# A two-stage graph network on one core: each graph layer sums its messages over the edge counts before the weight product, and the product out2 @ Wu is made of high and low parts

## What is computed

```python
# first stage
out1 = gat_conv(layer_norm(x), ..., W1, ...)          # 4 heads of 192
out2 = gat_conv(out1, ..., W2, ...)                   # 2 heads of 96
l0   = concatenate([x, out2], -1) @ Wu + bu
x1   = _layernorm(x + l0)
# second stage: gcn_conv twice
def gcn_conv(x, W, b):
    h = x @ W
    norm = dinv[src] * dinv[dst]                      # dinv = 1/sqrt(degree)
    return segment_sum(h[src] * norm[:, None], dst) + b
h   = relu(gcn_conv(x1, gW1, gb1))
out = _layernorm(x1 + gcn_conv(h, gW2, gb2))
```

## Time and profile before

| | |
|---|---|
| median of 3 runs | 818.07 us (817.19 to 819.74) |
| span of the profiled execution | 818.5 us |
| PE busy | 781.8 us, 96% |
| weight loads busy | 656.0 us, 80% |
| VectorE busy | 583.6 us, 71% |
| ScalarE busy | 301.9 us, 37% |
| GpSimd busy | 19.9 us, 2% |
| mean granted TensorE clock | 0.988 |

### The profile page before, as it was taken

One profiled execution on the slowest core, in us unless ns is written; L12 is line 12 of the kernel. 1 busy time (PEld: TensorE's weight loads), 2 busy tenths in 40 slices (PEclk: granted clock), 3 DMA queues, 4 the chain that ended last, 5 costly groups with the idle time before them and its releaser, 6 DMA issues. The chain is left out here.

```text
span 818.5 us, 11911 instructions
## 1 busy us (share of the span) xinstructions
PE 781.8 (96%) x4286; PEld 656.0 (80%) x4286; DVE 583.6 (71%) x1145; ACT 301.9 (37%) x622; POOL 19.9 (2%) x36
## 2 busy tenths in 40 slices
PE   5999999998999999999998999899999999999997
PEld 4966666665666989999766887788898889999997
DVE  2599997885999999999689998966616432113444
ACT  4546576654534334444154454222212311110000
POOL 6100000000000020000000000000000000000000
PEclk9999999999899999999999999999999999999999
DMA  9400000000000131010000500000021000000111
GB/s 310 155 2 1 1 2 1 1 2 1 1 1 0 66 131 65 1 65 1 1 0 22 188 1 2 1 1 1 1 99 38 1 1 1 1 1 20 59 58 54
DMA packets 10541, 27.78 MB, mean 34 GB/s; under 512 B 665, under 2 KB 4075, under 8 KB 9968
## 3 DMA queue, kind: packets, MB, share of 16 engines
q1 hardware_dynamic: 10480, 26.97, 9.4%
HBM read 23.09 MB, written 3.88 MB: 33 GB/s over the span
## 5 line engine op out<-in xcount | busy, mean ns | idle before, releaser
L1190 PE MATMUL ps<-g,att 128*128 128x193 f32 x800 | 133.5, 328 | 3.2 <-DVE att L662 1.8
L1190 PEld LDWEIGHTS ps<-g,att 128*128 128x128 f32 x800 | 130.4, 190 | 6.0 <-DVE att L662 3.3
L1025 ACT ACTIVATE att<-att,ssrc 128x1250 f32<-128x1250 f32 x60 | 80.2, 1338 | 97.8 <-DVE att L701 97.5
L701 DVE SCALAR_TENSOR_TENSOR att<-uB,s 128x1250 f32<-128x1250 f32 x60 | 90.4, 1511 | 0.0
L1190 PE MATMUL ps<-wp,xT 128*128 128x388 f32 x240 | 87.5, 502 | 0.8 <-ACT xT L908 0.8
L662 DVE SCALAR_TENSOR_TENSOR att<-att,ct 128x1250 f32<-128x1250 f32 x60 | 87.2, 1455 | 0.7 <-ACT att L1025 0.5
L1190 PE MATMUL ps<-yhi,ctr 128*128 128x384 f32 x200 | 67.7, 338 | 0.0
L1190 PEld LDWEIGHTS ps<-wp,xT 128*128 128x128 f32 x240 | 42.6, 190 | 24.8 <-issue 1.0
L765 DVE SCALAR_TENSOR_TENSOR ylo_a<-ps,dinv,yhi 128x384 fp32r<-128x384 f32 x32 | 18.9, 615 | 57.5 <-ACT yhi L883 57.4
L883 ACT ACTIVATE yhi<-ps,dinv 128x384 fp32r<-128x384 f32 x40 | 22.1, 580 | 86.8 <-PE ps L1190 86.8
L1190 PE MATMUL ps<-ylo_a,ctr 128*128 128x384 f32 x160 | 54.1, 338 | 0.0
(11 more groups left out here) (259 smaller groups left out, 1445.4 us busy)
## 6 DMA issues: line engine op xcount, KB each, us to landing
uB<-u_dram SPq DMA_DIRECT2D x4, 1280.0 KB, 6.0
wux<-in_L_gnn_Wu SPq DMA_DIRECT2D x2, 2304.0 KB, 15.7
gw<-in_L_gnn_W SPq DMA_DIRECT2D x2, 2304.0 KB, 10.9
xs<-in_x SPq DMA_DIRECT2D x1, 3456.0 KB
out<-ybuf SPq DMA_DIRECT2D x9, 384.0 KB, 2.3
w<-in_L_gnn_W SPq DMA_DIRECT2D x2, 1152.0 KB, 6.9
w2x<-in_L_gnn_W SPq DMA_DIRECT2D x1, 576.0 KB, 7.7
wuo<-in_L_gnn_Wu SPq DMA_DIRECT2D x1, 576.0 KB
```

Source lines behind the costliest of these rows:

```text
L701: v.scalar_tensor_tensor(att[:, att_place(n), 0:N], uB[:, hp % 2, 1, 0:N], s08[:, h, q:q + 1], uB[:, hp % 2, 0, 0:N], ALU.add, ALU.max).th ...
L1025: a.activation(at_, at_, ACT.Exp, bias=ssrc[:, h, q:q + 1]).then_inc(att_exp, 1)
L1190: return t.matmul(o, lhsT, rhs, start=start, stop=stop, **kw)
```

## The change

**Order of the layers.** Each layer sums its messages first and multiplies by the weights afterwards. The message of a tile is the normalised tile times dinv (`message_high` on ScalarE, `message_low` on VectorE); it has nodes on partitions already, so x1 is not transposed any more. The sums come out transposed and are split at once (`sums_high`, `sums_low`). The product with gW1 then has nodes on partitions, so the bias is a row that is broadcast (`gb1b`), and `degree_rows`, `sqB` and `dinv2` are not used. The last product before the epilogue is now h-sums @ gW2, 18 products for each half instead of 20.

**Order on PE at the start.** Per tile: `o_half`, the transposes of the next tile, `o_half`, then `pair` of the tile two before (LAG = 2), which sums slices 0 and 1 of the features. Slice 2 is summed for tiles 0 to 7 after that, then tiles 8 and 9 for slices 0 to 2, then slices 3 to 5. The wide branch is taken ahead of all this.

**out2 @ Wu.** Six fp32r products for each half of a tile in place of two plain fp32 ones. ScalarE makes the high parts of the weights in the last attention head, GpSimd the low parts; VectorE makes `o2Tlo`.

**Engines.** Widening the counts moves from VectorE to ScalarE. The low part of gW1 moves behind slice 2 of the sums. The ranges of windows are held as 16-bit integers.

```diff
+LAG = 2
+A_BANKS = [(2, 3, 4), (6, 7, 4), (0, 1, 5), (2, 3, 4), (6, 7, 0), (1, 5, 2)]
@@ sync
-            sp.wait_ge(y_ps, 2 * T)
+            sp.dma_start(gb1b[:, :], t_in["L1_gnn_b1"]...to_broadcast([P, D])).then_inc(gcn_in, 16)
+            sp.dma_start(gb2b[:, :], t_in["L1_gnn_b2"]...to_broadcast([P, D])).then_inc(gcn_in, 16)
+            sp.wait_ge(h_ps, 2 * T)
             sp.dma_start(gw2[:, :, :], ...)
@@ gpsimd
+            pool.wait_ge(wuo_hi, 2)
+            pool.tensor_tensor(wuolo[0:HC, 0, :], wuo[0:HC, 0, :], wuohi[0:HC, 0, :], ALU.subtract)
+            pool.tensor_tensor(wuolo[0:HC + 1, 1, :], wuo[0:HC + 1, 1, :], wuohi[0:HC + 1, 1, :], ALU.subtract)
@@ vector
+                o2t_low(0)
                 for q in range(T):
+                    residual(q)                 # two adds, o2t_low(q + 1) between them
+                    if q > 0:
+                        normalised(q - 1)
+                    variance(q)
+                    if q > 0:
+                        message_low(q - 1)
+                normalised(T - 1)
+                message_low(T - 1)
                 for f in range(KD):
+                    sums_low(f, a_place, ahi_out, alo_out)
+                    if f == 2:
+                        first_weight_low(0, KD)
@@ scalar
+                    if hp == H1 + 1 and q < 2:
+                        if q == 0:
+                            a.wait_ge(wuo_in, 32)
+                        copy(wuohi[0:HC + q, q, :], wuo[0:HC + q, q, :], wuo_hi)
+                o2_transposes(0)
+                o2_transposes(1)
+                count_tile(0)
+                count_tile(1)
+                deviation(0)
+                o2_transposes(2)
                 for q in range(T):
+                    message_high(q)
                     if q + 1 < T:
+                        deviation(q + 1)
                     if q + 3 < T:
                         o2_transposes(q + 3)
+                    count_tile(...)
+                def sums_high(f, place, sums_ps, done, last):
+                    a.wait_ge(sums_ps, last)    # last = max(3 * f + 3, 6) in the first layer
+                    for k, (c0, c1) in enumerate(PIECES):
+                        copy(yhi[...], place(f, k), done)
@@ tensor
-                mm(ps[:, k, 0:HALF], o2T[0:HC, ...], wuo[0:HC, 0, ...], True, False)
-                mm(ps[:, k, 0:HALF], o2T[0:HC + 1, ...], wuo[0:HC + 1, 1, ...], False, True)
+                for o in range(H2):
+                    mm(ps[:, k, 0:HALF], o2Thi[0:rows, q % 2, o, :], wuohi[0:rows, o, cols], o == 0, False)
+                    mm(ps[:, k, 0:HALF], o2Thi[0:rows, q % 2, o, :], wuolo[0:rows, o, cols], False, False)
+                    last = mm(ps[:, k, 0:HALF], o2Tlo[0:HC, q % 2, o, :], wuohi[0:HC, o, cols], False, o == 1)
+                for q in range(1, T):
+                    o_half(q, 0)
+                    if q + 1 < T:
+                        o2_transposes(q + 1)
+                    o_half(q, 1)
+                    if q >= LAG:
+                        pair(q - LAG)
+                for q in range(T - LAG):
+                    sums(2, q)
+                for q in range(T - LAG, T):
+                    pair(q)
+                    sums(2, q)
+                for f in range(3, KD):
+                    for q in range(T):
+                        sums(f, q)
```

More of the change, by code:

```diff
@@ L760, in _, with messages, o2t_low, residual @@
             v.wait_ge(att_used, (H1 + H2) * T)
[L762 to L768, removed]
-                steps = n_own[0]
[L771 to L775, removed]
+            def messages(y):
+                steps = n_own[0]
+                def o2t_low(q):
+                    v.wait_ge(o2t_out, q + 1)
+                    v.tensor_tensor(o2Tlo[0:HC, q % 2, :, :], ps[0:HC, 5, 0:2 * P].rearrange("p (o n) -> p o n", o=2),
+                                    o2Thi[0:HC, q % 2, :, :].bitcast(F32), ALU.subtract).then_inc(o2tlo_out, 1)
+                def residual(q):
                     for k in range(2):
+                        if k == 1 and q + 1 < T:
+                            o2t_low(q + 1)
                         v.wait_ge(o_ps, 2 * q + k + 1)
@@ L852, in first_end @@
+                hidden_low(2 * T - 1)
+                for f in range(KD):
+                    sums_low(f, b_place, bhi_out, blo_out)
+                    if f == 1:
                         for c in range(KD):
@@ new lines, in messages @@
+                for n in range(2 * T):
+                    q, k = n // 2, n % 2
+                    a.wait_ge(h_pre, n + 1)
+                    a.activation(hpre[:, n % 2, :], hpre[:, n % 2, :], ACT.Relu).then_inc(h_relu, 1)
+                    a.wait_ge(h_relu, n + 1)
+                    a.wait_ge(h_ps, 2 * q + 2)
+                    copy(ydst[:, q, k * HALF:(k + 1) * HALF], hpre[:, n % 2, :], h_out, scale=dinv[:, q:q + 1])
+                a.wait_ge(hlo_out, 2 * T)
+                for f in range(KD):
+                    sums_high(f, b_place, b_ps, bhi_out, 3 * f + 3)
+                    if f == 1:
@@ L1170, in messages @@
                             copy(gw2hi[:, c, :], gw2[:, c, :], gw2_hi)
-                ring = (6, 7, 0, 1)
-                for n in range(2 * T):
-                    q, k = n // 2, n % 2
-                    a.wait_ge(y2_ps, 2 * q + 2)
-                    copy(ydst[:, q, k * HALF:(k + 1) * HALF], ps[:, ring[n % 4], 0:HALF], y2_out, scale=dinv2[:, q:q + 1])
             with a.If(is_wide > 0):
-                messages(y32)
+                messages(ct32, y32)
             with a.Else():
-                messages(yhi)
+                messages(ctr, yhi)
             for q in range(T):
@@ L1519, in y_low @@
-            def y_low(k):
-                for c in range(KD):
-                    t.wait_ge(gw1_lo, c + 1)
-                    last = mm(ps[:, y_bank(k), 0:HALF], x1Thi[0][:, c, :], gw1lo[:, c, k * HALF:(k + 1) * HALF], False, c == KD - 1)
-                last.then_inc(y_ps, 1)
-            t.wait_ge(row_out, 2 + H1 + H2)
-            t.wait_ge(wuo_in, 32)
-            o2_transposes(0)
-            o_half(0, 0)
-            o2_transposes(1)
-            o_half(0, 1)
-            o_tile(1)
-            o2_transposes(2)
@@ L1614, in gcn @@
-                for n in range(2 * T):
-                    qd, k = n // 2, n % 2
-                    if n >= 4:
-                        t.wait_ge(f_out, n - 3)
-                    for q in range(T):
-                        if n == 0:
-                            t.wait_ge(y2lo_out, 2 * q + 2)
-                        for m, part in enumerate(parts):
-                            last = mm(ps[:, 2 + n % 4, 0:HALF], counts[:, q, qd * P:(qd + 1) * P], part(q, k * HALF, (k + 1) * HALF),
-                                      q == 0 and m == 0, q == T - 1 and m == len(parts) - 1)
-                    last.then_inc(f_ps, 1)
+                            t.wait_ge(blo_out, 3 * c + 1 + next(m for m, (_, c1) in enumerate(PIECES) if q * P < c1))
```

380 lines of the change are left out of this document (163 added, 217 removed).

## The result

The changed kernel takes 808.1 us (median of 4 runs, 807.23 to 809.86) against 817.63 us for the kernel before, measured beside it (median of 4, 816.88 to 819.74). The ratio is 0.9872, 95% interval 0.9846 to 0.9898: faster by 1.0 to 1.5%. Forecast were 810.6 us, range 806.5 to 816.5. The profiled execution of the changed kernel has a span of 807.0 us. In the fences PE is TensorE and DVE is VectorE.

A forecast was written before the change was run, and what follows sets the result against it. PE, busy 96% of 818.5 us, was taken as the bound. Less 14.3 us of PE work, plus 8.6 idle, less 4.3 idle before: 808.5; one clock fall of 2.5 gave 811.0 span, 810.6 us median, range 806.5 to 816.5.

The forecast's parts named there:

- The clock: After the start's gaps or the wait ahead of slice 3: one fall to half clock, 2.5 us, added to the span.
- the clock holds: Rival: the granted clock stays up through both new gaps, 808.5 us span, 808.1 us; chance 0.22.
- The point of departure: End of the second attention layer: VectorE ends at 506.9 us, so the first out2 @ Wu product was put at 507.9.
- The start: From 505.0 us to the end of `pair(0)` at 519.9: 14.9 us, 9.5 of work and 5.4 idle on PE.
- The round: Each message tile: PE needs 4.65 us, round about 4.75, 0.7 us idle over 7 rounds; bounds minus 0.7 and plus 3.2.
- fp32r on 96 and 97 rows: out2 @ Wu: 0.175 us per product, at most 0.194; twelve products take 2.10 us for 2.59, saving 4.9 over ten tiles.
- The wait ahead of slice 3: After the last pair, PE waits for banks to be emptied: about 2.5 us idle, bounds 1.5 and 3.5.
- Stages behind: From slice 3 to the last product: 34.9 + 63 + 69.7 + 63 us without a wait.
- GpSimd, at 0: Two 768-column subtractions from about 476 us, beside VectorE's two-input instructions, end by 507: cost 0, at most 2 us.
- the factor of 5.8: GpSimd's slowdown beside two-input VectorE instructions: 2.59 us against 0.45 alone for 128 columns, so 15.5 us per 768-column subtraction.

The follow-up runs named there:

- Kernel (2): Changed kernel with TensorE's branch taken before the last attention head, first transposes in front and 12 unread products filling its wait; 808.19 us, 0.9865.
- (3): Changed kernel with ScalarE's start reordered, TensorE's early branch, early transposes and 12 unread products, and slice 2 of tiles 4 to 9 behind the last pair; 802.63 us.
- the version without idle products: Kernel with ScalarE's start reordered, early branch and transposes, and late slice 2, minus its 12 unread products; 804.52 us, 0.9835 against the kernel before.

## Why the prediction was right, step by step

Faster, in the range, and the reason is the forecast one: PE's work fell and the rounds stayed PE's. Against the forecast span of 811.0 the profile has 807.0, 4.0 us less. That is made up so:

- **The clock, 2.5 us too much.** This is the term that failed. The forecast charged a fall on top of the idle times. A fall came where it was expected, behind the start's gap, but its 1.6 us lay beside ScalarE's chain and were not paid. Kernel (2), whose clock held there and fell one gap later, gained 0.1 us, less than two profiles of one kernel differ by. The kernel with plain fp32, whose clock held through its whole start, was no quicker to slice 0 (10.8 us against 11.0). With ScalarE's chain shortened, keeping the clock up gave 1.4 ((3) against the version without idle products). Idle time and half clock at one place must not be added; the later of the two chains counts. Behind the gap ahead of slice 3 the clock held in both profiles of the changed kernel. The rival "the clock holds" named 808.1 us, the very number measured, but its mechanism did not happen, the clock fell and was hidden; that the number fits is luck.
- **The point of departure, 0.9.** VectorE's last attention instruction stood at 505.42, not at 506.35. In the second profile it was at 504.09, and 1.27 of these 1.33 us stood already at the first attention product (261.41 and 260.14). That nothing of it comes from the smaller degree and bias inputs or the 16-bit window ranges at the start was not shown: those were not undone one by one. The spread between executions is larger than 0.9 us.
- **The start, 0.2 short.** First product 1.3 us after the end of VectorE's work (forecast 1.0), `pair(0)` ends 13.2 us after it (519.19; forecast 13.0). The sum came out by luck, its parts did not: 2.1 us of idle ahead of the third tile were forecast and 0.29 measured, since PE arrived late, through the branch (1.45 us idle, costed at nothing because PE "waits for VectorE anyway") and the half clock.
- **The round.** 4.65 us, the lower bound, for 4.75 taken: 0.7 less. VectorE's own pace is 4.14 (forecast 4.2 to 4.5), so PE never waits. `message_low` takes 1.01 us (0.95 taken from gw1lo), `message_high` 0.94 (0.9).
- **fp32r on 96 and 97 rows.** One product every 0.175 us, the row of the same width; the upper bound 0.194 was not needed. The split takes 0.49 us off each tile, 4.9 in all, and 3.3 us reached the median: the first three tiles' share lies in the start, where other chains than PE's bound the time (10.8 us to slice 0 without the split, 11.0 with it).
- **The wait ahead of slice 3.** 2.49 us for 2.5 forecast.
- **Stages behind.** 230.49 us from slice 3 on, for 34.9 + 63 + 69.7 + 63 = 230.6. The first gW1 product stands at 605.24 and gW2's at 737.88, none with a wait.
- **GpSimd, at 0.** The cost was right (0.2 us) by luck, by the place and not by the reason given. The working asked only whether GpSimd would be late. That a GpSimd instruction doubles a VectorE instruction beside it was left out, and only its last 0.4 us lay beside the next of VectorE's instructions with two SBUF inputs: ten microseconds later the same work costs 3 us. The 2.59 us of the earlier trace rows were also a wait and no slower rate: that subtraction ran from 298.09 to 300.68, and VectorE's instruction with two SBUF inputs beside it ended at 300.37. So the factor of 5.8, and with it 15.5 us for 768 columns, had no ground; 3.13 us is the most that was seen.

The profiled span stood 0.4 us above the median before, and 1.1 below it after, which takes 1.5 of the 4.0 back: 810.6 forecast, 808.1 measured.

## What to carry to other kernels

Where two chains of nearly one length meet, a loss on one (a branch, a half clock, a table load) costs nothing and its removal gives nothing until the other is shortened too: here 0.1 and 0.2 us alone, which the spread between executions covers, and 2.2 together. Work put on GpSimd must be costed on VectorE's side as well: if VectorE is the bound there and reads two SBUF operands, each GpSimd instruction can hold one of its instructions up for the whole of its own length. And when products are interleaved with what feeds them, the lag decides: one tile less of it cost 42 us here. The version with both starts and the late slices beats both kernels: 802.63 us, 0.9804 (0.9779 to 0.983).

## What the runs showed of the hardware that was not expected

- A subtraction of 768 columns on GpSimd takes 1.81 to 1.85 us alone and 2.9 to 3.1 beside VectorE instructions with two SBUF inputs, and those take 3.1 us instead of 1.5.
- At a branch past a large block of unused instructions TensorE idled 1.37 to 1.92 us in nine profiles; in the kernel before, at another place, it was 0.61. With the branch ahead of the last head and the first transposes ahead of the products, the first product came 0.6 us sooner. The Trainium skill (Runtime: NRT & Kernel Launch, Instruction fetch mechanics) says that a taken branch out of what has been fetched waits for a DMA of the target; the traces show the gap, not its cause.
- Twelve idle products of 384 columns, 2.1 us in a wait of that length, kept the granted clock at 1.00; without them it was 0.50 for some 3 us and the start took 1.4 us longer. In two of eleven profiles without them it held as well. The gap of 2.5 us ahead of slice 3 was followed by a fall in 3 of 10 profiles.
